# A batch's linear attention and MLP placed beside the experts of the batch before it

## The reference

```
x += ga * [ linear attention (16 heads, elu+1) and then an MLP 128-512-128 with Gelu, on norm(x)*(1+ca)+sa ]
x += gb * [ 8 dense experts, each Wd(silu(Wg h) * (Wu h)), 128-512-128, summed ]
x += ga1 * [ causal attention, 8 heads of 16 over the 512 tokens, a geometric bias in the scores ]
x += gb1 * [ 16 heads of 64 over 512 keys; each head's values are mixed from 8 projections by a top-2 gate,
             and its output goes through the top-2 of 8 output projections ]
```

## Time and profile before

| | us |
|---|---|
| median of 3 executions | 2928.8 |
| lowest, highest | 2925.64, 2928.84 |
| the profiled execution | 2925.12 |
| its span | 2923.4 |
| PE busy | 2399.3 (82%) |
| DVE busy | 1530.1 (52%) |
| ACT busy | 1339.4 (46%) |
| POOL busy | 769.2 (26%) |

### The profile page before, as it was taken

The page is one execution under the profiler, slowest core; times in us unless marked ns, Lnnn a source line. Parts: engine busy times, 40 slices in busy tenths (PEclk is TensorE's granted clock), DMA queues, the critical chain, the costliest instruction groups (busy, mean ns, idle before and its releaser), DMA issues.

```text
span 2923.4 us, 41764 instructions
## 1 busy us (share of the span) xinstructions
PE 2399.3 (82%) x15724; PEld 1397.4 (48%) x15724; DVE 1530.1 (52%) x2649; ACT 1339.4 (46%) x2923; POOL 769.2 (26%) x345
## 2 busy tenths in 40 slices
PE   3885798789897798878988798878988789896687
PEld 2333345554455444554455444554445444463465
DVE  4223583446734475454844558444663548547732
ACT  0223226463364624645255543645336452564364
POOL 1000560015500182011900137001640019205500
PEclk7876799899998999989999899999999899999799
DMA  2110110202010030101201121010201003001101
GB/s 78 43 51 1 26 47 1 59 15 70 22 44 15 16 85 7 45 15 44 63 1 44 30 58 34 22 38 15 70 22 45 15 24 82 1 16 33 23 25 39
DMA packets 210689, 101.15 MB, mean 35 GB/s; under 512 B 137367, under 2 KB 189620, under 8 KB 210492
## 3 DMA queue, kind: packets, MB, share of 16 engines
q1 hardware_dynamic: 205052, 95.74, 12.0%
q10 hardware_dynamic: 5440, 2.75, 0.4%
HBM read 77.48 MB, written 20.99 MB: 34 GB/s over the span
## 4 chain that ended last, share of the span: by engine, by line
PE 49%; ACT 11%; DVE 10%; issue 10%; POOL 6%; DMA 0%; ACTq 0%; DVEq 0%; POOLq 0%
PE bank L1036 10%; PE bank L744 10%; PE bank L1073 7%; POOL prod L729 5%; ACT prT L1242 3%; ACT pr L1255 3%; PE bank L856 3%; PE bank L859 3%; PE bank L864 3%; PE bank L896 2%; DVE prod L1542 2%; PE bank L1027 2%; PE bank L1048 2%; DVE nmax L1589 2%; PE bank L916 1%
## 5 line engine op out<-in xcount | busy, mean ns | idle before, releaser
L729 POOL TENSOR_TENSOR prod<-pv,mixv 128x1024 f32<-128x1024 f32 x190 | 609.6, 3248 | 229.3 <-ACT pv L1202 155.2
L1589 DVE TENSOR_REDUCE nmax<-bank 128x1 f32<-128x512 f32 x512 | 341.4, 686 | 578.9 <-PE bank L1036 578.9
L1242 ACT ACTIVATE prT<-bank 128x512 f32<-128x512 f32 x512 | 306.6, 599 | 602.1 <-PE bank L744 599.0
L1036 PE MATMUL bank<-keys,qs 64*128 64x512 f32 x896 | 285.2, 711 | 208.9 <-ACT pr L1255 92.8
L671 POOL TENSOR_TENSOR rstd<-vareps,minus_half 128x4 f32<-128x4 f32 x48 | 48.4, 1009 | 1367.1 <-DVE vareps L1350 1367.1
L1255 ACT ACTIVATE pr<-bank,nmax 128x512 f32<-128x512 f32 x512 | 350.6, 687 | 82.9 <-DVE nmax L1589 82.3
L744 PE MATMUL bank<-ident,pr 128*128 128x128 f32 x2048 | 351.1, 298 | 30.6 <-ACT prT L1242 29.7
L744 PEld LDWEIGHTS bank<-ident,pr 128*128 128x128 f32 x2048 | 241.4, 150 | 270.5 <-issue 259.4
L1140 ACT ACTIVATE arena<-bank 128x512 f32<-128x512 f32 x256 | 152.8, 597 | 471.4 <-PE bank L856 417.2
L1073 PE MATMUL bank<-prT,vals 128*64 128x128 f32 x3584 | 262.1, 291 | 55.1 <-ACT prT L1242 55.1
L1550 DVE TENSOR_REDUCE vals<-prod 128x128 f32<-128x1024 f32 x224 | 269.4, 1208 | 42.6 <-POOL prod L729 42.6
(11 more groups left out here) (234 smaller groups left out, 2933.4 us busy)
## 6 DMA issues: line engine op xcount, KB each, us to landing
Wg<-in_L_ffn_Wg SPq DMA_DIRECT2D x64, 256.0 KB, 2.7
Wu<-in_L_ffn_Wu SPq DMA_DIRECT2D x64, 256.0 KB, 3.1
Wd<-in_L_ffn_Wd SPq DMA_DIRECT2D x64, 256.0 KB, 3.8
out_rows<-on SPq DMA_DIRECT2D x32, 512.0 KB, 2.6
onR<-out_rows SPq DMA_DIRECT2D x32, 512.0 KB, 4.2
xin<-in_L_attn_x SPq DMA_DIRECT2D x8, 256.0 KB, 4.4
mask_rows<-masko SPq DMA_DIRECT2D x8, 256.0 KB, 4.5
maskR<-mask_rows SPq DMA_DIRECT2D x8, 256.0 KB, 6.7
```

Of the source, the lines that this page charges most:

```text
L729: g.tensor_tensor(*value_piece(n), ALU.mult).then_inc(vprod_r[0], 1)
L1036: pe.matmul(S[(turn + odd) % len(S)][:, :], qs[half, j % 3, r, :], keys[half, p, :], start=True, stop=True).then_inc(s_ps[0], 1)
L1242: s.activation(prT[:, m % 3, :], TP[m % len(TP)][:, :], ACT.Copy).then_inc(pT_r[0], 1)
L1589: v.tensor_reduce(nmax[:, m % NPR:m % NPR + 1], S[turn % len(S)][:, :], X_AXIS, ALU.max, negate=True).then_inc(nmax_r[0], 1)
```

## The change

- attn0 of batch b+2 now stands beside the experts of b+1, with the values of b. It has 20 marks: the MLP is one piece (mark 17), four fc1 products in three banks and then four fc2 products, and the four Gelus follow each other.
- It works in the banks of the heads, named A0, A1B, A2, A3 (S0, S1, TB, OB), after the heads of b-1 are closed, and in columns of `arena` that the experts don't use. Its transposed norm goes to a tile of its own (h1F), and h0 exists twice.
- A new stage, early, makes all eight keys (with hdT as input) and all four pv of batch b in F1 and F3, within the gates of b, beside the heads of b-1: 6 marks of two products and two copies. The matrix work of values and its copies go from the stage of values; pv and the keys have room for all and for two batches.
- picks now lies in `arena`, so the experts of b+1 wait on DVE (mix_g) and ACT (masko_r, mix_g) until the gates of b are done.
- DVE makes 4 of the 32 products instead of 8 (`VALUES_V`); the last batch's split stays.
- moe_in of b+1 comes behind early, within the gates; SP loads the first two experts' weights there instead of in load.
- The counts that the layer norms wait for follow from the new order (norm_at, turn_at); the layer norm on DVE also waits until PE has read the one before.

```diff
-MARKS = {"load": 1, "attn0": 24, "moe_in": 3, "experts": NE * NJ, "attn1": E1 + 6, "gates": 13,
+MARKS = {"load": 1, "attn0": 20, "moe_in": 3, "experts": NE * NJ, "attn1": E1 + 6, "gates": 13,
...
-VALUES_V = [n for n in range(NQ * NT) if n % 4 == 3]
+VALUES_V = [n for n in range(NQ * NT) if n % 8 == 5]
...
+MARKS["early"] = (NP + NT) // 2
...
+        A0, A1B, A2, A3 = S0, S1, TB, OB
...
+            def gates_and(b, *others):
+
+                both, rest = [], marks("gates", b, 1, MARKS["gates"])
+                for mark in [mark for part in others for mark in part]:
+                    both += rest[:1] + [mark]
+                    rest = rest[1:]
+                return both + rest
+
+            def between(b):
+
+                return gates_and(b, marks("early", b, 1, MARKS["early"]), marks("moe_in", b + 1, 1, MARKS["moe_in"]))
+
+            def beside_experts(b):
+
+                front = marks("load", b + 2, 1, 1) + marks("attn0", b + 2, 1, MARKS["attn0"]) if b + 2 < NB else []
+                some = CLOSE_BEHIND if b else 0
+                parts = front[:2]
+                if b:
+                    parts += of(("finish",), b - 1) + marks("values", b, 1, some) + front[2:4] + of(("close",), b - 1)
+                else:
+                    parts += front[2:4]
+                front = front[4:]
+                for m in range(some + 1, BEGIN_BEHIND + 1):
+                    parts += front[:1] + marks("values", b, m, m)
+                    front = front[1:]
+                return parts + front + of(("begin",), b) + marks("values", b, BEGIN_BEHIND + 1, MARKS["values"])
+
+            schedule(stages, [(of(("load", "attn0", "moe_in"), 0), []), (of(("experts",), 0), of(("load", "attn0"), 1)),
+                              (of(("attn1",), 0) + between(0), []), (of(("experts",), 1), beside_experts(0))])
             for b in range(1, NB - 1):
-                schedule(stages, [(of(("heads",), b, -1), fronts(b)), (of(("experts",), b, 1), after_heads(b, -1))])
+                schedule(stages, [(of(("heads",), b - 1), of(("attn1",), b) + between(b)),
+                                  (of(("experts",), b + 1), beside_experts(b))])
             last = NB - 1
-            at = (last, 0)
-            schedule(stages, [(of(("heads",), last - 1), of(FRONT_B, last) + [("values", at, range(1, LAST_BESIDE + 1))]),
-                              (of(("finish",), last - 1), [("values", at, range(LAST_BESIDE + 1, LAST_BESIDE + CLOSE_BEHIND + 1))]),
-                              (of(("close",), last - 1), [("values", at, range(LAST_BESIDE + CLOSE_BEHIND + 1, MARKS["values"]))]),
-                              (of(("begin",), last) + [("values", at, [MARKS["values"]])], []),
+            schedule(stages, [(of(("heads",), last - 1), of(("attn1",), last) + gates_and(last, marks("early", last, 1, MARKS["early"]))
+                               + marks("values", last, 1, LAST_BESIDE)),
+                              (of(("finish",), last - 1), marks("values", last, LAST_BESIDE + 1, LAST_BESIDE + CLOSE_BEHIND)),
+                              (of(("close",), last - 1), marks("values", last, LAST_BESIDE + CLOSE_BEHIND + 1, MARKS["values"] - 1)),
+                              (of(("begin",), last) + marks("values", last, MARKS["values"], MARKS["values"]), []),
...
                 wait(sp, WoutG_r, b, 0)
                 sp.dma_start(rows1a[:, :], row_table[bass.ds(b[0] + b[1], 1), 3 * P:4 * P].to_broadcast([P, P])).then_inc(rows1a_in[0], 16)
                 expert(b, 0)
                 expert(b, 1)
-                yield 1
+                yield MARKS["moe_in"]
 
             def values(b):
                 wait(sp, masko_r, b, 1)
...
-                        yield 17 + j
+                pe.wait_ge(ln_evac[0], turn_at(b, 2) + 1)
+                for j in range(NJ):
+                    if j == NJ - 1:
+                        wait(pe, hid_r, b, 1)
+                    pe.matmul((A2, A3, A0)[j % 3][:, :], fc1T[:, j * P:(j + 1) * P], h1F[:, :], start=True, stop=True).then_inc(fc1_ps[0], 1)
+                for j in range(NJ):
+                    wait(pe, hid_r, b, j + 1)
+                    last = pe.matmul(A1B[:, :], fc2T[:, j, :], hid[:, j, :], start=(j == 0), stop=(j == NJ - 1))
                 last.then_inc(fc2_ps[0], 1)
...
+            def early(b):
+
+                for n in range(NP + NT):
+                    f = (F1, F3)[n % 2]
+                    if n >= 2:
+                        if n - 2 < NP:
+                            wait(pe, keys_r, b, n - 1)
+                        else:
+                            wait(pe, pv_r, b, n - 1 - NP)
+                    if n < NP:
+                        pe.matmul(f[:, :], WkT[:, n * P:(n + 1) * P], hdT[:, :], start=True, stop=True).then_inc(k_ps[0], 1)
+                    else:
+                        i = n - NP
+                        pe.matmul(f[:, :], hdT[:, i * P:(i + 1) * P], WvT[:, :], start=True, stop=True).then_inc(pv_ps[0], 1)
+                    if n % 2:
+                        yield n // 2 + 1
...
             def experts(b):
+                wait(s, masko_r, b, 0)
+                wait(s, mix_g, b, 0)
...
+            def early(b):
+                for n in range(NP + NT):
+                    f = (F1, F3)[n % 2]
+                    if n < NP:
+                        wait(s, k_ps, b, n + 1)
+                        s.activation(keys[:, n, :], f[:, :], ACT.Copy).then_inc(keys_r[0], 1)
+                    else:
+                        wait(s, pv_ps, b, n - NP + 1)
+                        s.activation(pv[:, n - NP, :], f[:, :], ACT.Copy).then_inc(pv_r[0], 1)
+                    if n % 2:
+                        yield n // 2 + 1
+
+            def values(b):
+                if is_last(b):
+                    yield MARKS["values"]
+                s.activation(hdB[:, :], hdT[:, :], ACT.Copy).then_inc(hdB_r[0], 1)
+                yield NQ * NT // 2
+                wait(s, stored, b, 0)
+                wait(s, rden_r, b, 0)
...
+                v.wait_ge(ln_rstd[0], norm_at(b, n) + 1)
+                if turns_before(b, n):
+                    v.wait_ge(ln_T[0], turns_before(b, n))
                 for i in range(NT):
...
 
             def experts(b):
+                wait(v, mix_g, b, 0)
                 for n in range(NE * NJ):
```

More of the change, by code:

```diff
@@ L117, with norm_at, turn_at, turns_before @@
 LAST_BESIDE = 24
+def norm_at(b, n):
+    at = sum(b)
+    if n >= 4:
+        return 7 + 6 * at + n - 4 - (3 if at == NB - 1 else 0)
+    if n == 3:
+        return 6 * at + 3
+    return n if at == 0 else 6 * at - 2 + n
+def turn_at(b, n):
+    at = sum(b)
+    if n >= 4:
+        return 5 + 5 * at + n - 4 - (2 if at == NB - 1 else 0)
+    if n == 3:
+        return 5 * at + 2
+    return n - 1 if at == 0 else 5 * at - 2 + n - 1
+def turns_before(b, n):
+    return turn_at(b, n) if n else turn_at(b, 1)
 def weight(name, m):
@@ L285, in keys_of, with h0_of, behind @@
         def keys_of(b):
-            return keys_last if is_last(b) else keys_loop
+            return (keys_even, keys_odd)[sum(b) % 2]
+        def h0_of(b):
+            return h0s[sum(b) % 2]
+        def behind(b, k):
+            return (b[0] - k, b[1])
         def score_banks(b):
@@ new lines, in of, with marks @@
+            def of(names, b):
+                return [(name, (b, 0)) for name in names]
+            def marks(name, b, first, end):
+                return [(name, (b, 0), [m]) for m in range(first, end + 1)]
+            def gates_and(b, *others):
[4 more added lines that the diff above has]
+                return both + rest
@@ L624, in close @@
                 yield MARKS["close"]
-            program(sp, {"load": load, "experts": experts, "values": values, "heads": heads, "finish": finish, "close": close})
+            program(sp, {"load": load, "moe_in": moe_in, "experts": experts, "values": values, "heads": heads, "finish": finish, "close": close})
             sp.wait_ge(stored[0], 16 * NB)
@@ L798, in attn0 @@
                 for i in range(NT):
-                    last = pe.matmul(F0[:, 0:P + 1], ke[:, i, :], v0[:, i, :], start=(i == 0), stop=(i == NT - 1))
+                    last = pe.matmul(A0[:, 0:P + 1], ke[:, i, :], v0[:, i, :], start=(i == 0), stop=(i == NT - 1))
                 last.then_inc(kv_ps[0], 1)
@@ L1124, in attn0 @@
                     wait(s, fc1_ps, b, j + 1)
-                    s.activation(hid[:, j, :], (F2, F3)[j % 2][:, :], ACT.Gelu, bias=cols[:, 4 + j:5 + j]).then_inc(hid_r[0], 1)
-                    yield 17 + j
-                yield 24
+                    s.activation(hid[:, j, :], (A2, A3, A0)[j % 3][:, :], ACT.Gelu, bias=cols[:, 4 + j:5 + j]).then_inc(hid_r[0], 1)
+                yield 20
             def moe_in(b):
@@ L1175, in attn1 @@
                 yield E1 + 5
+                wait(s, k_ps, b, 0)
                 wait(s, pv_ps, b, 0)
@@ L1358, in attn0 @@
             def attn0(b):
-                wait(v, x5_r, b, 0)
```

(4 more changed lines are left out.)

237 lines of the change are left out of this document (83 added, 154 removed).

## The result

The changed kernel takes 2945.9 us (median of 5 executions, 2942.8 to 2954.3); the kernel before, run beside it, takes 2925.6 us (median of 5, 2919.4 to 2928.8). The ratio is 1.0075, 95% interval 1.0054 to 1.0095: slower by 20 us, more than the 0.2% that can be told from no change. I had forecast 2880 us and given "slower" 0.18: the direction was wrong, though the measured time still lies inside the upper edge of the 8-in-10 range (2795 to 2950). The profiled execution took 2944.5 us, span 2942.7.

A forecast was written before the change was run, and what follows sets the result against it. The heads' second part was taken as bound by a chain of hand-overs, the experts by PE and POOL. Terms -96 + 60 + 21 - 36 + 10 - 8 + 4 = -45 from 2925.1 gave 2880 us; 8-in-10 range 2795 to 2950.

The forecast's parts named there:

- slower: Whole kernel: the outcome of a longer time than the kernel before, given 0.18, all from the in-order queues.
- attn0 enters the experts' stage: Experts' stage: PE alone gives 115 us, POOL's path 120.6 against 108.1; +12 a stage, +60 for experts 2 to 6.
- The port: Experts' stage: norms and row operations beside POOL's products add 4.8 us a stage to POOL's path, 24 in all; left out.
- The spacing: Experts' stage: one POOL piece a round to the middle, two at the end; POOL's lead is late, its path 120.6 us.
- PE's hand-overs: Experts' stage: new hand-overs stop PE twice for 2.1 us, at elu's Exps and at att, 4.2 in all.
- attn0 leaves the heads' stage: Heads' stage, second part: 27.8 us a turn leave the chain, an upper bound; net of early -16, six times -96.
- early: Heads' stage: its 12 products count whole on PE, 10.6 us, plus some 1.5 of ACT's copies: +12 a turn.
- The rival of more gain: early fits PE's waits and POOL keeps its lead: heads -26, experts +7 a turn, 2787 us; chance 0.20.
- The ends: Outside the steady turns: experts of 0 +21, gates of 0 -36, experts of 1 +10, experts of 7 -8, heads of 6 +4.
- the in-order queues: Experts' stage: about ten new DVE waits precede products PE needs; a whole round each makes 3034 us; chance 0.18.
- The sign that I had named: Experts' stage: wrong if DVE idles before the experts' product for ACT, or PE for DVE, over 10 us a stage.
- Loads of a table: ACT: 1.28 us each, seven on the heads' chain for 8.9 us; the skill's 1.38 drain, giving about 2845, not counted.

The follow-up runs named there:

- experiment 1: Changed kernel, with POOL waiting after the second and third root until DVE's norm is written: 2886.4 us, 0.9838 of the kernel before.
- experiment 6: Changed kernel, with the second and third norm made on ACT instead of DVE, POOL not held back: 2909.6 us, 0.9935 of the kernel before.
- Experiment 2: Changed kernel, with attn0's marks merged evenly over those of values instead of one to one first: 2865.8 us, 0.9748 of the kernel before.
- experiment 3: Changed kernel with POOL waiting for the norms, the even merge, and DVE's 16-element operation reading one operand from the bank: 2829.7 us, 0.9667 of the kernel before.
- experiment 9: Kernel before, nothing moved, only the MLP in one piece with four Gelus in a run: 2909.8 us, 0.9920 of the kernel before.
- experiment 5: DVE makes 8 of 32 products: in the changed kernel 2941.0 us (1.0049); with POOL's waits, even merge and 16-element edit too, 2847.1 us (0.9721).

## Why the prediction was wrong

The seven experts' stages came out 133 us over my terms, the heads' stages 53 us under them, the beginning 16 under: 64 together, from the -45 forecast to the +19 measured.

**The step that failed** is "attn0 enters the experts' stage", +12 us: it measured +30. Two of its parts did.

- *The port.* I took the cost of POOL and DVE at one port as one on POOL's path (4.8 us a stage), and left it out of the sum since "no row of this case shows a norm beside a product". Both were wrong. A row did show a norm beside a long operation of POOL, the maximum of 2355 ns in line 1355; I had read the four pieces' time on the chain (1.12 us) and not the spread of all of them. And it is DVE that is held, for the whole of POOL's operation, with the experts' product behind it in its queue. The place is not a coincidence either: the norm starts when the root ends, and that is when POOL is free to start its next long operation. Experiments 1 and 6 take the collision away from either side, for 9.1 and 7.1 us a stage. The Trainium skill ("SBUF — State Buffer", Who interferes with whom) says that whichever of the two issues first has the shared pair for its whole instruction and the other is fully blocked, and names `tensor_scalar`, the form of the norm, among those that can ask for it. The runs agree, with 2.80 us for a piece of 0.34. The rule was in the prediction, with the wrong engine as its victim.
- *The spacing.* I saw that the marks give "one piece a round up to the middle, two at the end" and that POOL's lead would be late, and summed POOL's path to 120.6. In the trace the lead is lost earlier and by more: POOL waits 36.1 us for sums, for which I had counted none behind its start, and eight products stand in a row at the end. The addition of mark 14 starts 72.9 us into the stage (forecast 67.9), and from the root behind it to POOL's last product it is 61.3 us (forecast 48.2), with 14.3 of waits for sums in them. One of these, 6.6 us, is the MLP's run on PE, which I had called covered for ACT and not followed on to DVE and POOL. Experiment 2 gives 17.4 us back, 10.1 of them not by the collision of the norms.
- *PE's hand-overs* were about right: the stop for att is 1.7 us in the changed kernel, that for the Exps 2.9 us at most in experiment 3, against my 4.2 for the two. With both costs gone the stage is 119.4, where I had said 115 for PE.

**attn0 leaves the heads' stage**: I called 27.8 us an upper bound and took a net of -16. Net it measured -25.8, and as early costs at least 7.5, attn0 was worth 33 or more. I put the missing part down to what I left at nothing, "in this the clock counts for nothing": the clock stands at 0.98 and 1.00 instead of 0.93 and 0.91, worth some 10 us of PE time a turn, with 10 us fewer waits on PE beside it. This is read from the traces; no run changes the clock alone. My sum of pieces is in doubt, too: six of the loads of tables, of which it had seven at 8.9 us, bring 2.7 when the Gelus are put in one run (experiment 9). The rival of more gain had the heads' figure nearly right (-26) and the experts' wrong.

**early** at +12 may have the right size: 7.5 us measured for its columns beyond the eighth, and what the rest costs, the copies above all, is not separated.

**The ends.** The start with the experts of 0 (+12 for +21) and the gates of 0 (-43 for -36) came out better than said. The experts of 1 (+44 for +10) took 144.1 us; in experiment 3 they take 119.4, so most of it goes with the same two causes. The even spread alone leaves them at 138.6, with all their collisions. The experts of 7 gained nothing (109.3, predicted 97 to 100). No run was made for them, but the trace shows POOL at their end: it starts its fourth product, behind the first sum, 22 us into the stage (I had said 20), then waits 8.2 and 3.0 us more for sums, and makes its last 22 products without a pause:

```profile
2444.03 66.03 POOL L771 TENSOR_TENSOR prod<-pv,mixv 128x1024 f32<-128x1024 f32 x22 [2.98 <-DVE vals L1593]
```

With DVE making 8 products (experiment 5) they take 107.4 us for 109.3.

**The rivals.** Slower came by the mechanism of the in-order queues in part: DVE held ahead of the experts' product that PE needs. But I had priced it as waits for results, each a round long. The largest part of what held DVE was not a wait in the program: in the trace it is busy time. DVE is at 98.7 us against 80.3, of which the two norms have 11.1 where eight free pieces take 2.7, and the operation of 16 elements 2.5 where it takes 0.2; the rest is attn0's own work less four products. The sign that I had named did come: PE stops 19.5 us for DVE in the stage, against 4.6 before. The seven stages came out 19 us each over the forecast, well above the 6.4 from which I said that it decides; the heads gave back enough to make it +19 and not +72.

**Loads of a table.** The sum had counted them at 1.28 us where they stood on the chain. Experiment 9 falls by 16 to 31 us (the interval's ends) for 36 loads less, below 36 x 1.28 = 46 us. The drain that the Trainium skill adds ("ScalarE: Activation LUTs", What ACT_TABLE_LOAD costs), with which 36 loads would come to 96 us, shows in no row here. In the kernel before, where ACT has no other wait, a load starts 0.02 us behind the operation before it, and the next operation 0.01 us behind the load:

```profile
2017.82 0.69 ACT L1125 ACTIVATE arena<-bank,cols 128x512 f32<-128x512 f32 x1
2018.53 1.28 ACT L1255 ACT_TABLE_LOAD   x1
2019.82 0.69 ACT L1255 ACTIVATE pr<-bank,nmax 128x512 f32<-128x512 f32 x1
```

The times can't exclude it, as they hold the cost of the run too.

## What to carry to other kernels

Before short DVE operations are moved beside a row of long GpSimd ones, read the maximum of their durations, not the median: one piece at seven times its usual length shows the lock, and here its victim was the engine whose operations are short. Where GpSimd hands DVE a result (here a root), try to let it wait until DVE has used it; here a wait for 1.1 us of norm saved 9 us a stage. And when two lists are merged, spread the shorter over the whole of the longer: a pairing one to one until the shorter is used up left the tail to one engine here.

## What the hardware showed that I had not expected

- A DVE operation of 128x128 with scalar operands, 0.34 us alone, took up to 2.85 us beside POOL's product, and one of 16 elements 2.51 us for 0.23; POOL's product kept its 2.8 us. The profile counts the time as busy, so no view of waits names it.
- A pair of POOL products with the norm beside it took 5.49 us (at 1785.75), a pair with no held operation beside it 5.66 (at 1806.58): being the one that holds cost nothing.
- The granted clock fell where the stops were: 1.00 in the first 58 us of the experts' stage, 0.79 in the next 26 us, which have the stops of 1.7 and 9.1 us, and pairs of products of 1.9 us and more for 1.02 behind each. Of the 9.4 us that experiment 1 gained in this stage, 3 were PE's shorter busy time.

```profile
1735.00:1765.00 30.00, 27.31 (x86) 13.45 (x84) 25.96 (x35) 9.90 (x16) 19.52 (x8) 1.00 0.37 70
1765.00:1791.40 26.40, 16.46 (x39) 7.20 (x39) 18.65 (x28) 2.98 (x5) 13.89 (x7) 0.79 0.10 33
```
